# New orders of work on all five queues of a four-stage transformer kernel

## What is computed

```python
x = x + cross_attention_16_heads(layernorm(x), ctx, Wq, Wkv)            # layer 0
# layer 0, experts: 8 of them, top 2 by a gate, plus a shared product
probs = softmax(flat @ gate_W); w, idx = top_k(probs, 2)
out = 0.5 * gelu(flat @ shared_W + shared_b)
for e in range(8):
    out += combine[:, e] * (gelu(flat @ W1[e] + b1[e]) @ W2[e] + b2[e])
x = x + layernorm(out) * gamma + beta
# layer 1: attention with one head and a mask over the context
Z = (q @ Wq) @ (ctx @ Wk).T / 16;  Z = where(mask == 0, -1e9, Z)
x = x + softmax(Z) @ (ctx @ Wv)                                         # q = layernorm(x)
# layer 1, linear step on rows and weights rounded in blocks of 32 to a 6-bit grid
x = x + quantised(layernorm(x)) @ quantised(weight).T + bias
```

## Time and profile before

| | us |
|---|---|
| median of 3 runs | 1076.71 (1071.17 to 1078.43) |
| the profiled execution | 1070.92 |
| its span in the trace | 1069.1 |
| attention, first scores to last gate | 14.0 to 305 |
| routing and experts | 305 to 881 |
| second layer | 881 to 1069 |
| TensorE busy over the span | 945.4 (88%) |
| VectorE, ScalarE, POOL busy | 560.1, 497.1, 539.3 |

### The profile page before, as it was taken

The page is one execution under the profiler, slowest core; times in us unless marked ns, Lnnn a source line. Parts: engine busy times, 40 slices in busy tenths (PEclk is TensorE's granted clock), DMA queues, the critical chain, the costliest instruction groups (busy, mean ns, idle before and its releaser), DMA issues.

```text
span 1069.1 us, 21031 instructions
## 1 busy us (share of the span) xinstructions
PE 945.4 (88%) x7159; PEld 808.6 (76%) x7159; DVE 560.1 (52%) x1231; ACT 497.1 (46%) x1257; POOL 539.3 (50%) x654
## 2 busy tenths in 40 slices
PE   6999999999823699999999999999999989787776
PEld 4777777777612699999999999999999978554544
DVE  3888888888769223433223223322322313679882
ACT  3666666666642233333333333333333324666663
POOL 2333333333325455555565565555556532578883
PEclk9999999999955799999999999999999998999998
DMA  5434343433217521222221221222222244122201
GB/s 142 142 111 152 100 153 101 156 103 135 80 22 203 148 41 30 41 37 35 41 40 31 41 40 32 40 40 33 39 41 36 35 91 118 43 76 90 90 33 35
DMA packets 74709, 80.11 MB, mean 75 GB/s; under 512 B 12752, under 2 KB 69904, under 8 KB 74480
## 3 DMA queue, kind: packets, MB, share of 16 engines
q1 hardware_dynamic: 58704, 60.12, 18.6%
q0 software_dynamic: 15904, 18.66, 11.1%
HBM read 52.51 MB, written 26.25 MB: 74 GB/s over the span
## 4 chain that ended last, share of the span: by engine, by line
PE 60%; DVE 20%; issue 8%; POOL 6%; ACT 5%; DMA 2%; POOLq 0%; SPq 0%; DVEq 0%; ACTq 0%
PE b_H L1269 24%; PE b_Y L1281 23%; DVE a_max L635 5%; DVE a_probs L641 4%; PE a_T L506 2%; ACT a_probs L738 2%; PE a_S L496 2%; PE b_xT L1256 1%; PE c_g_ps L1940 1%; PE c_v_ps L1945 1%; POOL a_rstd L401 1%; PE c_f_ps L1911 1%; DVE a_xin L625 1%; ACT c_xn L1804 1%; DVE c_x L1773 1%
## 5 line engine op out<-in xcount | busy, mean ns | idle before, releaser
L1435 ACT ACTIVATE b_hiddenT<-b_H,b_b 128x128 f32<-128x128 f32 x568 | 162.4, 368 | 331.9 <-PE b_H L1269 331.9
L1269 PEld LDWEIGHTS b_H<-b_rowsT,b_w 128*128 128x128 f32 x2272 | 266.6, 193 | 6.0 <-ACT b_rowsT L1444 2.4
L1269 PE MATMUL b_H<-b_rowsT,b_w 128*128 128x128 f32 x2272 | 267.3, 276 | 1.8 <-ACT b_rowsT L1444 1.8
L1281 PE MATMUL b_Y<-w_sb,b_hiddenT 128*128 x1136 | 256.8, 379 | 0.0
L1227 POOL DMA_INDIRECT ffn_rows<-b_y,scatter_idx x71 | 154.0, 2169 | 193.7 <-DVE b_y L1360 185.2
L1281 PEld LDWEIGHTS b_Y<-w_sb,b_hiddenT 128*128 128x128 f32 x1136 | 210.5, 190 | 25.7
L1356 DVE TENSOR_TENSOR b_y<-b_Y,b_bc 128x256 f32<-128x256 f32 x71 | 30.2, 425 | 324.1 <-PE b_Y L1281 324.1
L1349 DVE COPY b_w<-w_sb 128x2048 f32 x71 | 87.1, 1227 | 37.5 <-issue 26.0
L635 DVE TENSOR_REDUCE a_max<-a_S 128x8 f32<-128x960 f32 x64 | 73.6, 1149 | 26.9 <-PE a_S L496 25.1
L1213 POOL DMA_INDIRECT b_rows<-xn_rows,gather_idx x71 | 73.5, 1035 | 21.5 <-issue 19.7
L744 ACT COPY a_probsT<-a_T 120x512 f32<-120x512 f32 x128 | 69.1, 594 | 28.1 <-PE a_T L506 28.1
(11 more groups left out here) (219 smaller groups left out, 1367.2 us busy)
## 6 DMA issues: line engine op xcount, KB each, us to landing
w_sb<-in_L_ffn_W SPq DMA_DIRECT2D x32, 512.0 KB, 4.5
a_xin<-in_x SPq DMA_DIRECT2D x16, 256.0 KB, 3.0
a_xres<-in_x SPq DMA_DIRECT2D x32, 128.0 KB, 2.0
xn_rows<-a_xn SPq DMA_DIRECT2D x32, 128.0 KB, 2.3
x_rows<-a_x SPq DMA_DIRECT2D x32, 128.0 KB, 2.0
ffn_rows<-shared SPq DMA_DIRECT2D x2, 2048.0 KB, 18.6
c_x<-x_rows SPq DMA_DIRECT2D x16, 256.0 KB, 2.7
c_acc<-ffn_rows SPq DMA_DIRECT2D x16, 256.0 KB, 2.7
```

Source lines behind the costliest of these rows:

```text
L1269: j = pe.matmul(H_ps[i][:, c * P:(c + 1) * P], w1c[i][:, k * HID + c * P:k * HID + (c + 1) * P], xT[:, k * P:(k + 1) * P], start=(k == 0), ...
L1281: j = pe.matmul(y_ps[i][:, 0:D], hT[i][:, c * P:(c + 1) * P], w2_sb[:, bass.ds(e * (HB * D) + c * D, D)], start=(c == 0), stop=(c == HB - 1))
L1435: j = act.activation(hT[i][:, c * P:(c + 1) * P], H_ps[i][:, c * P:(c + 1) * P], ACT.Gelu, bias=b1c[i][:, c:c + 1])
```

## The change

Both stages get new orders of steps on every engine, SP's queue in attention included. In attention the loop over tiles becomes a loop over batches with two tiles in each, with one order for the first and another for the second tile; steps of the tile before and two before are mixed in. The second layer's loops are reordered and reach one cycle further on either side; `project_context` and `keep_projected` are split into keys and values. `EARLY` goes from 8 to 7, and of the later contexts one is made in each cycle instead of two. Each step now returns at once where its batch or tile does not exist (the guards are left out below after the first). Waits are added where the new order no longer implies them.

```diff
@@ attention
+        CYCLES = range(-2, B + 2)
...
             def load_x(b):
+                if not batch(b):
+                    return
@@ SP
+            for b in CYCLES:
+                t = 2 * b
+                load_x(b + 2)
+                store_xn2(t - 3)
+                store_x2(t - 2)
+                load_ctx(b + 2)
+                if b == CYCLES[0]:
+                    load_weights()
+                load_residual(t + 1)
+                load_expert_weights(b)
+                store_x2(t - 1)
+                store_xn2(t - 2)
+                load_residual(t)
@@ POOL
+            for b in CYCLES:
+                t = 2 * b
+                residual(t - 2)
+                inverse_std2(t - 2)
+                residual(t - 1)
+                key_blocks(b + 1)
+                inverse_std2(t - 1)
+                add_beta(t - 2)
+                inverse_std1(b + 2)
+                add_beta(t - 1)
@@ TensorE
             def turn_context(b):
...
                 pe.wait_ge(s_ctx, 16 * b + 16)
+                ge(pe, s_ctxT, b)
+                ge(pe, s_T, 4 * (2 * b - 3) + 3)
...
             def weigh(t, q):
...
                 pe.wait_ge(s_T, 4 * t + q + 1)
+                if q == 0:
+                    pe.wait_ge(s_v, t // 2 + 1)
+                    ge(pe, s_oT, t)
+                    if batch(t // 2 + 1):
+                        pe.wait_ge((s_k, s_q)[t % 2], t // 2 + 2)
@@ TensorE
-            for t in range(TILES):
-                b, u = t // 2, t % 2
-                if tile(t - 1):
-                    turn_probs(t - 1, 2)
-                    turn_probs(t - 1, 3)
+            for b in CYCLES:
+                t = 2 * b
                 scores(t)
...
+                turn_probs(t - 1, 1)
+                weigh(t - 1, 0)
@@ VectorE
+            for b in CYCLES:
+                t = 2 * b
                 largest(t, 0)
                 less_max(t, 0)
+                normalise1(b + 1)
                 largest(t, 1)
+                keep_shared(t - 3)
                 less_max(t, 1)
+                stats2(t - 2)
+                over_sums(t - 1)
+                normalise2(t - 2)
+                largest(t + 1, 0)
+                stats2(t - 1)
+                less_max(t + 1, 0)
+                largest(t + 1, 1)
+                normalise2(t - 1)
+                keep_shared(t - 2)
+                less_max(t + 1, 1)
+                stats1(b + 2)
+                over_sums(t)
...
@@ second layer
-        CYCLES = range(-2, B + 2)
-        EARLY = 8
+        CYCLES = range(-3, B + 3)
+        EARLY = 7
@@ POOL
             for c in CYCLES:
+                scale_back(c - 2)
+                inverse_std(N4, c - 1, s_xn4)
+                inverse_std(N3, c + 1, s_xn3)
+                add_bias(c - 1)
+                to_blocks(c - 1)
+                inverse_std(NA, c + 3, s_x3)
@@ VectorE
             for c in CYCLES:
+                bounded(c)
+                stats_acc(c + 3)
+                residual(c + 2)
+                scales(c - 1)
+                stats_x3(c + 2)
+                attended(c)
+                stats_x4(c)
+                centre(c + 3)
@@ ScalarE
             for c in CYCLES:
+                n = c + EARLY
+                exps(c)
+                normalise_x4(c - 1)
+                if late(n + 2):
+                    keep_keys(n + 2)
+                keep_probsT(c)
+                normalise_x3(c + 1)
+                keep_result(c - 2)
+                if late(n + 3) and n + 3 > EARLY:
+                    keep_context(n + 3)
+                round_blocks(c - 1)
+                keep_xnT(c + 1)
+                if late(n + 1):
+                    keep_values(n + 1)
+                keep_xdT(c - 1)
```

More of the change, by code:

```diff
@@ L488, in scores @@
             def scores(t):
+                if not tile(t):
+                    return
                 b, u = t // 2, t % 2
@@ L611, in vector @@
+                weigh(t, 2)
+                shared_gate(t - 2)
+                weigh(t, 3)
+                values(b + 1)
+                queries(b + 1)
+                turn_probs(t + 1, 0)
+                turn_back(t)
         def vector(dve):
             def stats1(b):
+                if not batch(b):
+                    return
                 dve.wait_ge(s_xin, 16 * b + 16)
```

478 lines of the change are left out of this document (241 added, 237 removed).

## The result

| | before | after |
|---|---|---|
| median, us | 1075.02 (1071.17 to 1078.43, 4 runs) | 1039.45 (1037.02 to 1042.59, 4 runs) |
| profiled execution, and its span | 1070.92, 1069.1 | 1038.78, 1037.0 |
| ratio, 95% interval | | 0.9676 (0.9643 to 0.9708) |

The account below looks back on a forecast made before the run. TensorE was to bound attention, POOL's loop the second layer. Attention's -7 and the second layer's -18 us gave 1046 from the profiled 1070.9, 1052 from the median 1076.7; it took 1049 us, range 1036 to 1062.

Parts of the forecast that it names:

- a stretch: Attention, TensorE: each run of partial-array work costs 0.28 us going in and out; nine a batch instead of four.
- The base: Attention, TensorE: 16.0 us of work a batch, the 17.53 us period less 1.5 us of waits.
- the switches: Attention, TensorE: added changes between partial-array and full-array work cost 1.3 us a batch, giving a 17.3 us period.
- The edges: Attention's start and end: TensorE waits about 3 us in the first cycle and 1.5 at the end.
- Rival 4: Attention, SP's queue: residual load behind a store lands late, costing about 1.3 us a batch, 20 us; chance 0.03.
- the +0.8: Before the second layer's score steps: seven contexts in front instead of eight save nothing; 0.8 us is added.
- POOL's 0.57: Second layer: POOL's 0.57 us wait a cycle for the statistics of x4 goes, making the cycle 8.3 us.
- its 0.47: Second layer: POOL's 0.47 us wait a cycle for the block scales stays, as the scale step meets POOL's bias addition.
- no more than POOL's: Second layer: the loop through weighing, linear step and VectorE's steps takes 8.3 us, no longer than POOL's.
- 1: Rival, attention: added switches are free, TensorE's 16.0 us bounds the period; 20 us more gained, 1029 us; chance 0.1.
- 3: Rival, attention: switches cost their upper bound, 1.4 us more a batch; 20 us back, 1069 us; chance 0.07.
- 2: Rival, second layer: a new wait replaces the old and the cycle stays 8.87 us; 8 us back, 1057; chance 0.2.

## Why the prediction was right, and where its terms were off

**Attention, first scores to last weighing: the mechanism right, the closeness of the sum luck.** 274.4 us (13.12 to 287.5) against 274. In the steady period the waits went, TensorE is the bound, and a stretch costs 0.29 against my 0.28. Two terms were off and cancel. The base: 17.03 less 1.3 for the switches leaves 15.7 us of own work, not 16.0; by the same difference the waits before were 1.8 us, not 1.5. Over 16 batches that is 4.3 us less. The edges: at 17.03 my sum would give 269.8, so the first cycle and the end took 4.6 us more than my 4.5. The waits there are near what I had (2.75 us for the first rows, 1.61 and 0.35 at the end). What I had not priced is the granted clock behind the first of them, 0.51 for 6.3 us; eight key steps took 1.90 us there instead of 1.06:

```profile
17.30:23.60 6.30, 6.28 (x36) 5.33 (x36) 2.19 (x2) 3.51 (x7) 0.00 (x0) 0.51 0.51 145
```

**Behind the last weighing: missed, +3.9.** This stretch took 13.4 us here and 10.4 to 13.0 in the seven other kernels with this order of loads, against 9.4 before, so a part of the 3.9 is this execution's own. Rival 4 named the mechanism (the residual load behind other transfers) and looked for it in the steady batches, where it has about the slack I gave it: POOL waits for the load (until 171.09 us in the period from 165.93), but VectorE reads the sum only at 172.83, 1.0 us after POOL is done. It shows once, at the end, where no work of a next batch covers it and the load took 6.90 us, not 2.0.

**Experts: +3.8, not in the forecast, and not due to the change alone.** The second expert tile starts behind a wait of 3.53 us for its turned rows, 1.28 before, and takes 5.47 us instead of 3.84 for 32 products, at little over half the granted clock. The two differences, 2.25 and 1.63, are the 3.8. The timelines of before and after, and the changed kernel's busy table there (clock 0.56):

```profile
362.84 3.84 PE L1269 MATMUL b_H<-b_rowsT,b_w 128*128 128x128 f32 x32 [1.28 <-ACT b_rowsT L1444]
```

```profile
360.04 5.47 PE L1316 MATMUL b_H<-b_rowsT,b_w 128*128 128x128 f32 x32 [3.53 <-ACT b_rowsT L1491]
```

```profile
361.00:364.00 3.00, 3.00 (x18) 3.00 (x18) 0.17 (x2) 1.14 (x4) 0.00 (x0) 0.56 0.00 0
```

Four other kernels with the new attention did the ten tiles in about 75 us, with waits of 0.67 to 1.28 us there, and seven of all twelve in about 79, with 2.49 to 4.20. So this is no fixed price of the change; whether the change makes the long wait more frequent, and what decides it, stays open.

**In front of the score steps: wrong, -5.2 instead of +0.8.** The step that failed is the +0.8: I priced only the contexts and overlooked a wait that the change moves. Before, ScalarE waited for POOL's constant c_tie ahead of its first context copy; the change waits for it ahead of `round_blocks`, its only use. The timelines of before, TensorE and ScalarE, and its busy table (clock 0.50):

```profile
881.43 0.40 PE L1919 MATMUL c_ctxT_ps<-ident,c_ctx 120*128 120x120 f32 x2 [4.70 <-ACT c_ctxT L1824]
881.67 1.69 PE L1940 MATMUL c_g_ps<-c_ctxT,c_wkq 128*128 128x120 f32 x8
```

```profile
880.93 0.36 ACT L1824 COPY c_ctxT<-c_ctxT_ps 128x240 f32<-128x240 f32 x1 [8.83 <-POOL c_tie L1695]
```

```profile
882.00:885.00 3.00, 3.00 (x12) 2.49 (x12) 0.00 (x0) 0.59 (x2) 0.00 (x0) 0.50 0.44 106
```

and TensorE in the changed kernel:

```profile
876.10 0.40 PE L2014 MATMUL c_ctxT_ps<-ident,c_ctx 120*128 120x120 f32 x2 [0.54 <-ACT c_ctxT L1903]
876.33 1.06 PE L2035 MATMUL c_g_ps<-c_ctxT,c_wkq 128*128 128x120 f32 x8
```

The wait was 4.16 us longer, and behind the idle time TensorE ran its first context at half clock, 3.42 us instead of 1.97. With one context fewer in front (1.97) that is 7.6 us. Some 4.1 go back to the context work that now stands between the early contexts and the first turned rows (keys of two, values of one, and a wait of 0.80), and 1.6 come from shorter waits behind it: 5.1 or 5.2 in all. Both kernels with the second layer of before show the wait as well (4.75 and 4.77 us), the others do not; no run moved it alone, so that it is the cause is read from the waits, not tested.

**The cycle: direction right, size off, 7.98 instead of 8.3.** Removing POOL's 0.57 and keeping its 0.47 was right. The mis-sized term is POOL's loop: its own work, 8.87 - 0.57 - 0.47 = 7.83 us, which I took over as fixed. It came down to 7.51. Beside VectorE's centring two small steps took 0.40 and 0.80 us in the kernel before:

```profile
953.47 0.40 POOL L1660 TENSOR_SCALAR c_acc_ve<-c_acc_mv 128x2 f32<-128x2 f32 x1
953.95 0.80 POOL L1665 TENSOR_TENSOR c_acc_rstd<-c_acc_ve,c_minus_half 128x2 f32<-128x2 f32 x1
```

They now stand beside `attended` (which takes one operand from the matmul's result) and the statistics behind it, and take 0.22 and 0.71: 0.27 of the 0.32 us. With the centring back in its old place the first of them took 0.39 again; the second kept its 0.71, so its 0.09 stays unexplained. Both durations were in the trace, and I did not read a moved VectorE step as something that changes its neighbour on POOL. With its wait of 0.47 POOL still fills the cycle, but the chain of waits no longer runs through it: it runs through VectorE and ScalarE at 7.98, a loop that I had at "no more than POOL's" 8.3. One piece of my sum for it can be checked: weighing ends 4.8 us after the score step (951.72 to 956.53), not 5.5. The two loops are close: where the bias addition came first, the chain ran through POOL at 8.0. Each of four small moves made the cycle longer. The Trainium skill, "SBUF — State Buffer", section Who interferes with whom, has the rule for the scale step, a VectorE and a GpSimd step that exclude each other. The runs agree with it there: 0.17 us away from the bias addition, 0.43 to 1.15 beside it. But the 7 us that the forecast saw behind that wait were not to be had: where the scale step was kept clear of the bias addition, the cycle was 8.0 us or more.

**The other distances.** 14 times 0.32 is 4.5 us, the first distance 6.57 instead of 7.5 makes 0.9 more: together the 5.3 by which the term was off (118.35 against 123.7). The end is 1.4 us shorter instead of 0.6 longer. Three kernels with the same second layer have 23.1 us there, 0.2 longer than before, so this trace alone does not decide that term.

**Rivals.** 1 and 3 fell (a stretch costs 0.29 us). 2 fell for the order of the change and shows what it guarded against in the two kernels with another order, 8.85 and 8.97 us. 4 happened in small.

**In all.** The parts miss by -0.1, +3.9, -1.8, +3.8, -6.0, -5.3 and -2.0 us, 7.5 together. That the total lies inside the range rests in part on misses of both signs: without the two of +3.9 and +3.8 the time would be near 1032, below it.

## What to carry to other kernels

Read a reordering also by who runs beside whom: a step that moves changes the duration of what the other engines do at its old and at its new place. Look at every wait that a diff moves, not only at those it adds, and ask at the edges of a stage what it waits for: the largest miss here lies where one wait for a constant was moved. Where two loops of a cycle are within half a microsecond of each other, as here, a single moved step won nothing in four tries. And before a time is put down to an edit, look how much the same code varies between traces.

## What the runs showed of the hardware

- Changing between partial-array and full-array work cost TensorE 0.29 us a stretch, in and out together (2.55 us with two stretches, 2.26 with one, start against start, for the same steps).
- VectorE's 128x256 centring beside POOL's 128x512 product took 1.58 us for two instead of 0.96, and the product 1.14 instead of 1.05.
- A fall of TensorE's granted clock can lengthen a cycle that TensorE does not bound: at 0.81 a cycle took 9.0 us instead of 8.0. It need not: in the kernel before a cycle at 0.81 kept its 8.86 us. The busy time alone did not foretell it: 5.9 us in 8.0 was followed by 0.81 in one kernel and by 1.00 in another. Behind a wait of 3.53 us in front of the experts' second tile, of 4.70 in front of the second context's turn and of 2.75 at the start of attention it was 0.56, 0.50 and 0.51.
- The same load of 128 KB that lands in 2.3 us as a median took 6.9 at the end of attention, where it was issued 1.5 us behind a load of 512 KB; the ones issued ahead of the 512 KB loads took 2.2 to 2.4 there.
